# Causal attention with an int8 feed-forward on eight cores: scores and outputs issued in groups of two tiles, and VectorE's long work taken from a list

## The chip, the cores and the metric

One Trainium2 chip. The program runs on all 8 cores, each on one sequence of the batch, and no core waits for another. The time of a run is that of the slowest core, in device microseconds (us); a kernel's time is the median of its runs.

## What is computed

Per core, x is 2048 tokens by 1024 features. The reference, cut to one layer:

```
q = (x @ Wq.T) * 64 ** -0.5 ; k = x @ Wk.T ; v = x @ Wv.T      # 16 heads of 64
s = q @ k.T
attn = where(causal, 1 + s + 0.5 * s * s, 0)                   # no exponential
o = (attn @ v) / (attn.sum(-1) + 1e-6)
x = layernorm(x + o @ Wo.T)
x_scale = max(abs(x), -1) / 127 ; x_q = round(x / x_scale)
x = layernorm(x + (x_q @ weight_q.T) * x_scale * weight_scale + bias)
```

The kernel writes 1 + s + s²/2 as (s/√2 + 1/√2)² + 1/2: ScalarE squares the scores on their way out of PSUM, and the 1/2 comes in as a product of block sums of v with a step matrix.

## The kernel before

One Python program writes a queue of instructions for each engine; the engines run their queues in order and meet by semaphores. What stands earlier in an engine's queue is done earlier, so the order in which the program calls its functions is the schedule.

Attention runs in five stages, `GROUPS`: queries 0 to 511, 512 to 1023 and 1024 to 1535 (stages 0, 1, 2, width 512), then 1536 to 1791 and 1792 to 2047 (stages 3a and 3b, width 256). In each, 8 pairs of heads follow one another, and a pair has 3, 7, 11, 7 or 8 tiles of keys. A tile has two halves of TensorE work:

- `scores` (L458): two matmuls of 64 rows and up to 512 columns, one for each head of the pair, placed in the upper and the lower half of the array (`tile_position`), into one of two PSUM tiles `ps`. ScalarE's square (L470) empties it into `u`, one of 4 buffers. Tiles on the diagonal, up to three for a pair, get a causal mask from VectorE (L477), called 1.0 us of planned time later.
- `outputs` (L514): two matmuls of 128 rows onto `oab`, preceded on a pair's first tile by the constant's (L497). After a pair's last tile `finish` copies `oab` out (L572, L573, L576), sends the row sums through SP's DMAs for a reciprocal and a broadcast (L578 to L593), and GpSimd multiplies (L597).

The outputs of tile j are issued behind the scores of tile j+3 (`LOOK`). Between them `drive` puts other TensorE work, the filling: the projections of the next stage (K, Q, V items), and for the stage before the output projection (`out_proj`, item a), the transposes of its integers (`turn`, t) and the feed-forward (`ffn`, f). All are groups of 8 matmuls of 512 columns (`mm8`, L288) into two PSUM banks `fb`, which VectorE empties: the eviction. An order written out by hand, `orders`, lists the items of each stage, and `drive` hands them out two matmuls ("slots") at a time, in proportion to the tiles done; after a pair's last outputs `END_FILL` lets 4 more through.

Work that must come some time later is entered in `later` by `at(delay, fn)` against a planned clock, which gains `STEP_US` for a tile and `SLOT_US` for a slot. `run_until` takes entries out early when something needs them. After `out_proj(t)` VectorE runs the largest and smallest of each row (L669, L670), then for a pair of tiles short statistics (`chain1`), a root on ScalarE, `scales`, and the integers of both tiles (L721, `quantize`); `turn` adds bias (L749), `ffn` empties its banks with two operations a half (L768, L772); `chain2`, a root and `final` (L805) end with the store. All of these enter VectorE's queue at the call.

After stage 3b the last two tiles, 14 and 15, go through the same steps in a tail that is written out by hand.

Of the kernel before, what the change touches and what calls it, by code (L numbers as in the profile page):

```python
# [39 lines left out]
LOOK = 3  # L40
END_FILL = 4
NB = 6
STEP_US = 0.86
SLOT_US = 0.215
QRING = 8
NX1 = 4
# [70 lines left out]
def build_nc():  # L117
# [185 lines left out]
    def proj_qk(c, p, which):  # L303
# [25 lines left out]
        bank["free"][bi] = tok  # L329

    def proj_v(c, tt, half):
# [17 lines left out]
        bank["free"][bi] = tok  # L349

# [35 lines left out]
    clock = {"now": 0.0, "n": 0}  # L386
# [7 lines left out]
    def run_later():  # L394
        while later and later[0][0] <= clock["now"]:
            later.pop(0)[2]()

    def run_until(there):
        while not there():
            clock["now"] = max(clock["now"], later[0][0])  # L400
            later.pop(0)[2]()

# [30 lines left out]
    def attention(grp):  # L433
# [171 lines left out]

        for j in range(len(seq) + LOOK):
            if j < len(seq):
                scores(*seq[j])
            if j >= LOOK:
                outputs(*seq[j - LOOK])  # L610

            yield END_FILL if width == 512 and j >= LOOK and seq[j - LOOK][1] == seq[j - LOOK][2] - 1 else 0
# [25 lines left out]
    def load_tile(t):  # L638
        buf, b = home(t)
        if t < NT - 4:  # L640
            run_until(lambda: t >= NX1 or t + 2 in t_norm)
            waits = [t_out.get(t - NX1), t_norm[t + 2] if t < NX1 else None]
        else:
            waits = [t_vdone[0]]
# [10 lines left out]
    def out_proj(t):  # L655
# [3 lines left out]
        for half in range(2):  # L659
# [9 lines left out]
        P.op("vector", lambda e: e.reduce_max(MX(t, t + 1), buf[:, :], AX.X), [tok], inc=False)  # L669
        t_chain[t] = P.op("vector", lambda e: e.tensor_reduce(  # L670
            MN(t, t + 1), buf[:, :], AX.X, ALU.min))

        def square():
# [3 lines left out]
            if t % 2:  # L677
                at(3.5, lambda: chain1(t - 1, 2))
# [3 lines left out]
    def chain1(t0, n):  # L682
# [12 lines left out]
        def root():  # L695
            ts = P.op("scalar", lambda e: e.activation(
                V1(a, b), V1(a, b), AF.Sqrt, bias=c_eps), [tv])
            at(1.8, lambda: scales(ts, t))
# [16 lines left out]
    def quantize():  # L715

        while quant[0] in t_mm2 and (quant[0] < 2 or quant[0] - 2 in t_tr):
            k = quant[0]
            quant[0] += 1
            buf, _ = home(k)  # L720
            t_xq[k] = P.op("vector", lambda e, k=k, buf=buf: e.tensor_scalar(  # L721
                xq[k % 2][:, :], buf[:, :], S2(k, k + 1), MM2(k, k + 1), ALU.mult, ALU.add),
                [t_mm2[k], t_tr.get(k - 2)])

    def turn(t):
# [16 lines left out]
        def back():  # L742
# [6 lines left out]
        t_xb[t] = P.op("vector", lambda e: e.scalar_tensor_tensor(  # L749
            buf[:, :], buf[:, :], V1(t, t + 1), biasb[:, :], ALU.mult, ALU.add),  # L750
            [t_xq[t], tok_c["biasb"]])

    def ffn(t):
# [3 lines left out]
        for half in range(2):  # L757
# [9 lines left out]
            xh = buf[:, half * 512:(half + 1) * 512]  # L767
            t1 = P.op("vector", lambda e, bk=bk, half=half: e.scalar_tensor_tensor(  # L768
# [5 lines left out]
            bank["free"][bi] = tok  # L774
        t_r2[t] = tok

        def square():
# [3 lines left out]
            if t % 2:  # L781
                at(2.5, lambda: chain2(t - 1, 2))
# [3 lines left out]
    def chain2(t0, n):  # L786
# [9 lines left out]
        def root():  # L796
            ts = P.op("scalar", lambda e: e.activation(
                D1(a, b), D1(a, b), AF.Sqrt, bias=c_eps), [tv])
            at(1.0, lambda: final(ts))

        def final(ts):
            t = V(lambda e: e.reciprocal(D1(a, b), D1(a, b)), [ts])
            for k in range(a, b):
                buf, bf = home(k)
                tf = P.op("vector", lambda e, k=k, buf=buf: e.tensor_scalar(  # L805
                    buf[:, :], buf[:, :], M1(k, k + 1), D1(k, k + 1), ALU.subtract, ALU.mult), [t])
                t_out[k] = P.dma("sync", lambda e, k=k, buf=buf: e.dma_start(
                    d_out[k * 128:(k + 1) * 128, :], buf[:, :]), sem_ou[bf], [tf])
# [47 lines left out]
    def drive(main, steps, fill, total):  # L856
# [3 lines left out]
        for i, more in enumerate(main):  # L860
            clock["now"] += STEP_US
            run_later()
            while live and given < total * (i + 1) / steps + more:
# [39 lines left out]
    for grp, (c, first, width) in enumerate(GROUPS):  # L903
# [3 lines left out]
        steps = NP * len(u_tiles(c, first, width)) + LOOK  # L907
# [8 lines left out]
    run_until(lambda: not later)  # L916
# [208 lines left out]
```

How the kernel before makes its waits and increments, by code:

```python
        def play(eng, todo):  # L101
            for waits, fn, sem, k in todo:
                for s, v in waits:
                    eng.wait_ge(s.h, v)
                inst = fn(eng)
                if sem is not None:
                    inst.then_inc(sem.h, k)
```

## Time and profile before

| | |
|---|---|
| median of 3 runs | 662.59 us (655.40 to 665.08) |
| profiled execution | 665.16 us |
| its span, slowest core (core 2) | 663.6 us |
| other cores | 642.6 to 656.3 us |
| TensorE matmul busy | 601.0 us (91%), 3335 matmuls |
| TensorE weight load | 246.0 us (37%) |
| ScalarE busy | 371.2 us (56%) |
| VectorE busy | 344.2 us (52%) |
| mean granted clock, core 2 | 0.929 |

The span runs from the first instruction of a core to its last; the profiled execution's own time has about 1.5 us around it. A matmul's end is modelled and reaches over the next one's start, so TensorE's real pace is read from one start to the next. Stage 0 begins at 72 us on core 2, stage 1 at 151, stage 2 at 302, 3a at 452, 3b at 531 and ends at about 623.

### The profile page before, as it was taken

The numbers are of one execution on the slowest core, as the hardware profiler recorded it, in microseconds if no ns is written. First come the engines' busy times: TensorE is split into PE (matmuls) and PEld (weight loads), VectorE is DVE, ScalarE is ACT, GpSimd is POOL, SyncE is SP. The second block draws the span as 40 slices with busy tenths as digits, with TensorE's granted clock in tenths as the row PEclk, the third lists the DMA queues.
The fourth block names the chain that finished last, engine by engine and source line by source line (L and its number), as shares of the span: only waits on it lengthen the run. The fifth ranks groups of instructions, "written<-read, shape, count | busy, mean of one in ns | idle before, by whom it ended". The sixth has DMA issues, their size and how long they took to land.

```text
span 663.6 us, 10428 instructions; the slowest of 8 cores (642.6 to 663.6 us)
## 1 busy us (share of the span) xinstructions
PE 601.0 (91%) x3335; PEld 246.0 (37%) x3335; DVE 344.2 (52%) x773; ACT 371.2 (56%) x419; POOL 101.5 (15%) x147
## 2 busy tenths in 40 slices
PE   2989999999689889999999989999999978989973
PEld 0333333343223324333333333334445434444531
DVE  0324344553146766642376756453467744564585
ACT  0000333324336557546677768767889778998533
POOL 9100111121411111123210100012000120000000
PEclk9988888888769889999999989999999979999998
DMA  8996297725751224457721002133100140002011
GB/s 108 162 153 103 34 131 102 129 62 136 157 122 57 65 48 110 104 112 126 196 43 40 16 25 89 39 90 120 52 20 25 49 178 13 19 22 81 21 64 64
DMA packets 34276, 54.53 MB, mean 82 GB/s; under 512 B 10736, under 2 KB 13616, under 8 KB 34224
## 3 DMA queue, kind: packets, MB, share of 16 engines
q0 software_dynamic: 14976, 31.46, 26.8%
q1 hardware_dynamic: 19248, 22.41, 11.5%
q8 instruction: 28, 0.46, 0.3%
q14 instruction: 24, 0.20, 0.1%
HBM read 61.00 MB, written 8.52 MB: 105 GB/s over the span
## 4 chain that ended last, share of the span: by engine, by line
PE 61%; DMA 13%; DVE 10%; issue 7%; ACT 4%; SPq 3%; POOL 2%; DVEq 0%; ACTq 0%; POOLq 0%
PE fb L288 30%; PE oab L514 16%; PE ps L458 11%; DMA wv_sb<-wv 4%; DMA zscr<-zg 4%; DMA zg<-x 2%; PE oab L497 2%; ACT u L470 2%; DMA rzb<-zscr 2%; DMA zg<-osb 1%; DVE fb L768 1%; DVE xq L721 1%; SPq L593 1%; DVE u L477 1%; POOL wk_sb L230 1%
## 5 line engine op out<-in xcount | busy, mean ns | idle before, releaser
L470 ACT ACTIVATE u<-ps,consts 128x1024 f16<-128x1024 f32 (+2 forms) x288 | 303.5, 1066 | 173.1 <-PE ps L458 170.5
L514 PE MATMUL oab<-u,vx 128*128 128x256 f16 (+3 forms) x864 | 175.7, 311 | 1.1 <-DVE u L477 1.1
L458 PE MATMUL ps<-qT,kT 64*128 64x256 f16 (+3 forms) x864 | 112.5, 312 | 1.0 <-ACT u L470 0.7
L477 DVE SCALAR_TENSOR_TENSOR u<-u,cst_sb 128x256 f16<-128x256 f16 (+1 forms) x88 | 51.9, 591 | 79.4 <-ACT u L470 79.1
L514 PEld LDWEIGHTS oab<-u,vx 128*128 128x128 f16 x864 | 63.4, 99 | 63.8 <-issue 53.5
L597 POOL TENSOR_TENSOR slot<-osb,rzb 128x512 f16<-128x512 f32 (+1 forms) x35 | 39.2, 1120 | 291.8 <-DMA rzb<-zscr 278.9
L288 PE MATMUL fb<-wv_sb,slot 128*128 128x512 f16 x256 | 70.6, 414 | 6.2 <-DMA wv_sb<-wv 4.1
L458 PEld LDWEIGHTS ps<-qT,kT 64*128 64x128 f16 x864 | 30.5, 94 | 123.2 <-issue 122.1
L288 PE MATMUL fb<-wo_sb,slot 128*128 128x512 f16 x224 | 64.7, 397 | 11.7 <-POOL slot L597 8.4
L288 PE MATMUL fb<-wf_sb,xqT 128*128 128x512 f16 x224 | 63.0, 388 | 9.3 <-DVE stat L792 3.6
L288 PE MATMUL fb<-slot,wr 128*128 128x512 f16 x256 | 69.9, 394 | 1.4 <-DVE qT L326 1.4
L288 PE MATMUL fb<-slot,wk_sb 128*128 128x512 f16 x128 | 35.6, 431 | 13.0 <-DMA slot<-xT 12.7
L321 DVE CAST kT<-fb 128x512 f16<-128x512 f32 x32 | 22.1, 689 | 44.8 <-PE fb L288 44.7
L470 ACT ACT_TABLE_LOAD x1 | 1.3, 1283 | 72.7 <-PE ps L458 72.7
L288 PEld LDWEIGHTS fb<-wv_sb,slot 128*128 128x128 f16 x256 | 26.3, 104 | 40.9 <-issue 26.6
L288 PE MATMUL fb<-slot,wq_sb 128*128 128x512 f16 x128 | 36.2, 436 | 0.7 <-DVE qT L326 0.6
L288 PEld LDWEIGHTS fb<-slot,wr 128*128 128x128 f16 x256 | 24.7, 100 | 29.5 <-issue 12.5
L288 PEld LDWEIGHTS fb<-wo_sb,slot 128*128 128x128 f16 x224 | 22.5, 101 | 30.8 <-issue 19.2
L326 DVE TENSOR_SCALAR qT<-fb 128x512 f16<-128x512 f32 x32 | 21.9, 684 | 18.9 <-PE fb L288 18.6
L288 PEld LDWEIGHTS fb<-wf_sb,xqT 128*128 128x128 f16 x224 | 21.5, 99 | 25.6 <-issue 11.9
L666 DVE SCALAR_TENSOR_TENSOR x<-fb,x 128x512 f32<-128x512 f32 x24 | 16.5, 688 | 26.9 <-PE fb L288 26.8
L573 DVE COPY osb<-oab 128x512 f32<-128x512 f32 x20 | 13.8, 691 | 24.3 <-PE oab L514 21.2
(146 smaller groups left out, 521.5 us busy)
## 6 DMA issues: line engine op xcount, KB each, us to landing
rzb<-zscr SPq DMA_DIRECT2D x48, 128.0 KB, 2.9
x<-x_tok POOLq DMA_DIRECT2D x12, 512.0 KB, 7.7
out<-x SPq DMA_DIRECT2D x12, 512.0 KB, 3.4
slot<-xT POOLq DMA_DIRECT2D x16, 256.0 KB, 7.9
wr<-wk POOLq DMA_DIRECT2D x16, 256.0 KB, 5.3
wr<-wq POOLq DMA_DIRECT2D x16, 256.0 KB, 6.4
osb<-osb SPq DMA_DIRECT2D x20, 128.0 KB, 2.3
wk_sb<-wk POOLq DMA_DIRECT2D x8, 256.0 KB, 14.8
```

The lines of the kernel that those rows point to most:

```text
L230: tok_w[(0, name, j)] = tok_w[(1, name, j)] = P.dma("gpsimd", lambda e: e.dma_start(dst[:, j * D:(j + 1) * D], src[j]), s)
L288: tok = P.op("tensor", lambda e, lhs=lhs, rhs=rhs, i=i: e.matmul(out, lhs, rhs, start=(i == 0), stop=(i == n - 1)), list(w) + (list(waits) ...
L321: tok = P.op("vector", lambda e: e.tensor_copy(dst, bk[:, :]), [box[0]])
L326: tok = P.op("vector", lambda e: e.tensor_scalar(dst, bk[:, :], QSCALE, None, ALU.mult), [box[0], t_slast.get(c * NP + p - QRING)])
L458: tok = P.op("tensor", lambda e, r=r, kt=kt, qo=qo, w=w, col=col, ab=ab: e.matmul(pt[:, ab * 512 + col: ab * 512 + col + w], kT[r:r + 64, ...
L470: tok = P.op("scalar", lambda e: e.activation(dst, src, AF.Square, bias=c_rs, scale=RSQRT2), [t_s[g], t_o.get(g - NU), t_const])
L477: t_u[g] = P.op("vector", lambda e: e.scalar_tensor_tensor(ud, ud, 0.5, tri2[:, None, 0:diag].broadcast_to([128, 2, diag]), ALU.add, ALU.m ...
L497: t_oconst[c] = P.op("tensor", lambda e, ab=ab, base=base: e.matmul(oab[:, at_ab[ab]: at_ab[ab] + width], bs[c % 2][:, base: base + 128], ...
L514: tok = P.op("tensor", lambda e, base=base, qo=qo, w=w, col=col, ab=ab, end=end: e.matmul(oab[:, at_ab[ab] + qo: at_ab[ab] + qo + w], vx[: ...
L573: tb = t_oev[1] = P.op("vector", lambda e: e.tensor_copy(osb[b][:, 512:1024], oab[:, 512:1024]), [tok, before])
L597: t_norm[k] = P.op("gpsimd", lambda e: e.tensor_tensor(slot[o_slot[c]][:, p * 512 + first: p * 512 + first + width], osb[b][:, 0:width], r ...
L666: tok = P.op("vector", lambda e, bk=bk, xh=xh, acc=acc: e.scalar_tensor_tensor(xh, bk, 1.0, xh, ALU.mult, ALU.add, accum_out=acc), [box[0] ...
```

## The change

Tiles of one pair of heads are taken in groups of two (the last is alone where their number is odd). A group's scores are issued together, then the filling for both, then the outputs of the group before. `LOOK` and `END_FILL` are gone. VectorE's long operations, and the short statistics at each end of ScalarE's root except `root` itself, go into a second list, `idle`, in order of a rank; each eviction of the filling takes one entry out behind it, and so does a planned 2.2 us in which none was taken. The store of each tile is now split from its neighbour's, `load_tile` waits in the program until the buffer's store has been issued, and a planned tile costs 0.76 us instead of 0.86.

```
 NU = 4
-LOOK = 3
-END_FILL = 4
 NB = 6
-STEP_US = 0.86
+STEP_US = 0.76
 SLOT_US = 0.215
+IDLE_US = 2.2
 QRING = 8
...
         bank["free"][bi] = tok
+        evicted()
...
         bank["free"][bi] = tok
+        evicted()
...
-    clock = {"now": 0.0, "n": 0}
+    clock = {"now": 0.0, "n": 0, "idle": 0.0}
     later = []
...
             later.pop(0)[2]()
+        if idle and clock["now"] - clock["idle"] >= IDLE_US:
+            run_idle()
...
         while not there():
+            if idle and (not later or later[0][0] > clock["now"]):
+                run_idle()
+                continue
             clock["now"] = max(clock["now"], later[0][0])
...
+    idle = []
+    def when_idle(rank, fn):
+        idle.append((rank, clock["n"], fn))
+        clock["n"] += 1
+        idle.sort(key=lambda x: x[:2])
+    def run_idle():
+        clock["idle"] = clock["now"]
+        idle.pop(0)[2]()
+    def evicted():
+        if idle:
+            run_idle()
...
-        for j in range(len(seq) + LOOK):
-            if j < len(seq):
-                scores(*seq[j])
-            if j >= LOOK:
-                outputs(*seq[j - LOOK])
-            yield END_FILL if width == 512 and j >= LOOK and seq[j - LOOK][1] == seq[j - LOOK][2] - 1 else 0
+        groups = []
+        for p in range(NP):
+            mine = [x for x in seq if x[0] == p]
+            groups += [mine[i:i + 2] for i in range(0, len(mine), 2)]
+        before = []
+        for group in groups:
+            for x in group:
+                scores(*x)
+            yield len(group)
+            for x in before:
+                outputs(*x)
+            before = group
+        for x in before:
+            outputs(*x)
...
         if t < NT - 4:
-            run_until(lambda: t >= NX1 or t + 2 in t_norm)
+            run_until(lambda: t - NX1 in t_out if t >= NX1 else t + 2 in t_norm)
             waits = [t_out.get(t - NX1), t_norm[t + 2] if t < NX1 else None]
...
             bank["free"][bi] = tok
-        P.op("vector", lambda e: e.reduce_max(MX(t, t + 1), buf[:, :], AX.X), [tok], inc=False)
-        t_chain[t] = P.op("vector", lambda e: e.tensor_reduce(
-            MN(t, t + 1), buf[:, :], AX.X, ALU.min))
+            if half == 0:
+                evicted()
+        def largest():
+            P.op("vector", lambda e: e.reduce_max(MX(t, t + 1), buf[:, :], AX.X), [tok], inc=False)
+        def smallest():
+            t_chain[t] = P.op("vector", lambda e: e.tensor_reduce(
+                MN(t, t + 1), buf[:, :], AX.X, ALU.min), [tok])
+            if t % 2:
+                if t in t_sq1:
+                    when_idle(0, lambda: chain1(t - 1, 2))
+        when_idle(0, largest)
+        when_idle(0, smallest)
+        evicted()
...
             t_junk[0] = t_sq1[t]
-            if t % 2:
-                at(3.5, lambda: chain1(t - 1, 2))
+            if t % 2 and t in t_chain:
+                at(1.2, lambda: when_idle(0, lambda: chain1(t - 1, 2)))
...
                 V1(a, b), V1(a, b), AF.Sqrt, bias=c_eps), [tv])
-            at(1.8, lambda: scales(ts, t))
+            at(1.8, lambda: when_idle(0, lambda: scales(ts, t)))
...
             quant[0] += 1
-            buf, _ = home(k)
-            t_xq[k] = P.op("vector", lambda e, k=k, buf=buf: e.tensor_scalar(
-                xq[k % 2][:, :], buf[:, :], S2(k, k + 1), MM2(k, k + 1), ALU.mult, ALU.add),
-                [t_mm2[k], t_tr.get(k - 2)])
+            def integers(k=k):
+                buf, _ = home(k)
+                t_xq[k] = P.op("vector", lambda e: e.tensor_scalar(
+                    xq[k % 2][:, :], buf[:, :], S2(k, k + 1), MM2(k, k + 1), ALU.mult, ALU.add),
+                    [t_mm2[k], t_tr.get(k - 2)])
+            when_idle(0, integers)
...
         at(0.5, back)
-        t_xb[t] = P.op("vector", lambda e: e.scalar_tensor_tensor(
-            buf[:, :], buf[:, :], V1(t, t + 1), biasb[:, :], ALU.mult, ALU.add),
-            [t_xq[t], tok_c["biasb"]])
+        def bias():
+            t_xb[t] = P.op("vector", lambda e: e.scalar_tensor_tensor(
+                buf[:, :], buf[:, :], V1(t, t + 1), biasb[:, :], ALU.mult, ALU.add),
+                [t_xq[t], tok_c["biasb"]])
+        when_idle(1, bias)
...
             xh = buf[:, half * 512:(half + 1) * 512]
+            run_until(lambda: t in t_xb)
             t1 = P.op("vector", lambda e, bk=bk, half=half: e.scalar_tensor_tensor(
...
             bank["free"][bi] = tok
+            evicted()
         t_r2[t] = tok
...
             if t % 2:
-                at(2.5, lambda: chain2(t - 1, 2))
+                at(1.2, lambda: when_idle(2, lambda: chain2(t - 1, 2)))
...
                 D1(a, b), D1(a, b), AF.Sqrt, bias=c_eps), [tv])
-            at(1.0, lambda: final(ts))
-        def final(ts):
-            t = V(lambda e: e.reciprocal(D1(a, b), D1(a, b)), [ts])
             for k in range(a, b):
-                buf, bf = home(k)
-                tf = P.op("vector", lambda e, k=k, buf=buf: e.tensor_scalar(
-                    buf[:, :], buf[:, :], M1(k, k + 1), D1(k, k + 1), ALU.subtract, ALU.mult), [t])
-                t_out[k] = P.dma("sync", lambda e, k=k, buf=buf: e.dma_start(
-                    d_out[k * 128:(k + 1) * 128, :], buf[:, :]), sem_ou[bf], [tf])
+                at(1.0, lambda k=k: when_idle(2, lambda: final(k, ts)))
+        def final(k, ts):
+            t = V(lambda e: e.reciprocal(D1(k, k + 1), D1(k, k + 1)), [ts])
+            buf, bf = home(k)
+            tf = P.op("vector", lambda e: e.tensor_scalar(
+                buf[:, :], buf[:, :], M1(k, k + 1), D1(k, k + 1), ALU.subtract, ALU.mult), [t])
+            t_out[k] = P.dma("sync", lambda e: e.dma_start(
+                d_out[k * 128:(k + 1) * 128, :], buf[:, :]), sem_ou[bf], [tf])
...
         live = True
-        for i, more in enumerate(main):
-            clock["now"] += STEP_US
+        made = 0
+        for n in main:
+            made += n
+            clock["now"] += STEP_US * n
             run_later()
-            while live and given < total * (i + 1) / steps + more:
+            while live and given < total * made / steps:
                 w = next(fill, None)
...
         total = sum(cost.get(it[0], 0) for it in orders[grp].split())
-        steps = NP * len(u_tiles(c, first, width)) + LOOK
+        steps = NP * len(u_tiles(c, first, width))
         drive(attention(grp), steps if grp < len(GROUPS) - 1 else steps - 8, phase(c, orders[grp]), total)
...
     bank["n"] = 0
-    run_until(lambda: not later)
+    run_until(lambda: not later and not idle)
     V = lambda fn, w=(): P.op("vector", fn, w)
```

## Rows read from the trace of the kernel before

**Rows 1.** Spans and mean granted clock, three of the eight cores.
```profile
core 2: 663.6 us, clock 0.929
core 3: 656.3 us, clock 0.934
core 4: 642.6 us, clock 0.968
```

**Rows 2.** Core 2 by stage: stretch, length, busy us of each engine.
```profile
72.00:151.00 79.00, 78.97 (x355) 30.63 (x355) 40.32 (x83) 28.52 (x33) 15.17 (x23) 0.81 0.61 96
190.00:302.00 112.00, 104.98 (x522) 40.32 (x521) 71.53 (x168) 62.08 (x75) 19.06 (x25) 0.94 0.37 84
302.00:452.00 150.00, 145.16 (x738) 52.65 (x738) 82.94 (x180) 109.75 (x120) 20.27 (x23) 0.99 0.29 71
452.00:531.00 79.00, 78.27 (x617) 38.57 (x616) 45.67 (x106) 66.10 (x72) 9.48 (x12) 1.00 0.18 56
531.00:614.00 83.00, 74.46 (x586) 35.74 (x584) 43.35 (x97) 70.90 (x77) 7.02 (x10) 0.96 0.18 62
```

**Rows 3.** Timeline of TensorE: start, us, line, shapes, count.
```profile
306.65 0.59 PE L288 MATMUL fb<-slot,wr 128*128 128x512 f16 x2
307.18 0.39 PE L458 MATMUL ps<-qT,kT 64*128 64x512 f16 x2
307.50 0.60 PE L514 MATMUL oab<-u,vx 128*128 128x512 f16 x2
...
307.95 1.03 PE L288 MATMUL fb<-slot,wr 128*128 128x512 f16 x4
308.91 0.39 PE L458 MATMUL ps<-qT,kT 64*128 64x512 f16 x2
...
316.56 0.39 PE L458 MATMUL ps<-qT,kT 64*128 64x128 f16 x4
316.88 0.39 PE L514 MATMUL oab<-u,vx 128*128 128x512 f16 x1
```

**Rows 4.** What TensorE waited for: us in total, times, longest.
```profile
PE fb L288 <- POOL slot L597: 8.4, 2, 8.1
PE fb L288 <- DVE vx L347: 4.8, 4, 2.4
PE fb L288 <- DVE stat L792: 3.6, 1, 3.6
PE fb L288 <- ACT xqT L743: 3.0, 2, 1.6
PE fb L288 <- DVE x L772: 2.9, 2, 1.9
```

**Rows 5.** Timeline: VectorE's integers, an eviction behind them, TensorE's wait.
```profile
216.96 1.53 DVE L721 TENSOR_SCALAR xq<-x,stat 128x1024 f16<-128x1024 f32 x2
...
218.42 0.42 DVE L346 CAST vx<-fb 128x256 f16<-128x256 f32 x1
...
219.31 2.10 PE L288 MATMUL fb<-wo_sb,slot 128*128 128x512 f16 x7 [2.36 <-DVE vx L347]
```

**Rows 6.** The stretch after that wait, granted clock behind POOL's column.
```profile
220.40:223.80 3.40, 3.40 (x10) 0.94 (x9) 1.76 (x3) 1.11 (x1) 1.26 (x1) 0.50 0.22 54
```

**Rows 7.** Core 4: the last norm of group 0 and TensorE (timeline).
```profile
167.96 1.26 POOL L597 TENSOR_TENSOR slot<-osb,rzb 128x512 f16<-128x512 f32 x1 [5.59 <-DMA rzb<-zscr]
...
169.36 0.58 PE L288 MATMUL fb<-wo_sb,slot 128*128 128x512 f16 x1 [6.55 <-POOL slot L597]
```

**Rows 8.** ScalarE's squares, grouped by form: busy, mean ns, idle before.
```profile
L470 ACT ACTIVATE u<-ps,consts 128x1024 f16<-128x1024 f32 x248 | 273.9, 1114 | 150.8 <-PE ps L458 148.8 <-PE oab L514 0.6
```

**Rows 9.** VectorE's masks, grouped by form.
```profile
L477 DVE SCALAR_TENSOR_TENSOR u<-u,cst_sb 128x256 f16<-128x256 f16 x48 | 23.2, 483 | 48.6 <-ACT u L470 48.3
```

**Rows 10.** Timeline: integers of tiles 12 and 13, first transposes.
```profile
585.60 1.54 DVE L721 TENSOR_SCALAR xq<-x1l,stat 128x1024 f16<-128x1024 f32 x2
...
586.56 0.38 PE L732 MATMUL fb<-cst_sb,xq 128*128 128x128 f16 x4 [0.27 <-DVE xq L721]
```

## Prediction, made before the changed kernel ran

> **What bounds the kernel now.** I read the spans first: core 2 ends last at 663.6 us with a mean granted clock of 0.929, core 4 needs 642.6 at 0.968 [rows 1]. The difference arises early. Core 2 is granted 0.81 from 72 to 151 us [rows 2], and the cores come together again at a wait that no TensorE work shortens: the output projection of stage 0 needs the norm of the last pair of heads, whose DMAs land late. On core 4 GpSimd waits 5.59 us for them and TensorE 6.55 us in the last of its waits there, and it goes on at 169.4 us [rows 7]; core 2, which comes later, still waits 8.1 us [rows 4]. So TensorE time saved ahead of that point (185 us on core 2) is given back.
>
> Behind it, by the table of stages, TensorE is busy 105 of 112, 145 of 150, 78 of 79 and 74 of 83 us [rows 2]. ScalarE is next: 110 of 150 us in stage 2, 66 of 79 in 3a and 71 of 83 in 3b. VectorE never passes 72 of 112. TensorE bounds the kernel from 185 to about 614 us, and ScalarE is near enough in stage 3 to limit what TensorE can gain.
>
> What TensorE spends is in the timeline [rows 3]. Two filling matmuls take 306.65 to 307.18, 0.53 us; four take 307.95 to 308.91, 0.96 us. So one takes 0.215 us, and each run of them that ends in scores 0.10 us on top. The scores take 0.32 us (307.18 to 307.50, 308.91 to 309.23). Their two matmuls lie in different halves of the array and overlap, so the pass itself is one matmul long, 0.215, and 0.105 is on top again. The four score matmuls from 316.56, 512 columns in each half, also take 0.32: within scores nothing is paid for the next matmul. The pattern is a toll of about 0.105 us at each change between half-array and whole-array matmuls, in both directions; the table of instructions shows none of it as idle.
>
> The Trainium skill, page TensorEngine Tiling (Array Packing), section Key Properties, says that changing the tiling mode, not just the tile, drains TensorE. The trace agrees, with 0.10 and 0.11 us; without that rule the same rows could be a cost of each score tile, and grouping would save nothing (a rival, below).
>
> **Part 1, groups of two.** A pair has 3, 7, 11, 7, 8 tiles and gets 2, 4, 6, 4, 4 groups. Changes of mode before: 2 x 8 x 36 = 576. After: 2 x 8 x 20 = 320. Removed by stage: 16, 48, 80, 48, 64. At 0.105 us: 1.7, 5.0, 8.4, 5.0, 6.7, in sum 26.9 us. What of it counts:
> - stage 0 and the first 10 or so of stage 1's 56 tiles lie ahead of the wait for the norm: 0. Rest of stage 1: 46/56 x 5.0 = 4.1.
> - stage 2: 8.4. ScalarE stays at 110 of some 140 us.
> - stage 3a: ScalarE's 66 us fit in 79 - 5 = 74, but at 89% a queue of two squares will sometimes be late: 4.5.
> - stage 3b: the last pair has no filling; there a tile is 0.32 + 0.10 + 0.43 = 0.85 us of TensorE against 1.11 us of a square [rows 8], so its 8 changes are worth nothing. Of the other 56 x 0.105 = 5.9 I take 5.0.
> That makes 22.0, between 12.5 (stage 3 wholly at ScalarE's pace) and 24.3.
>
> Does the new order wait for squares? A group's second scores need the square of the preceding group's second tile. From those scores' end to that need TensorE has the filling, two outputs and one score tile: 1.3 us plus the filling. ScalarE needs both squares, 2.2 us, less the 0.2 by which it began earlier, plus some 0.2 of hand-over: 2.2. So the filling must last 0.9 us for a group. Stage 1 has 340 slots for 56 tiles, 2.6 us a group; stage 2 308 for 88, 1.5; 3a 132 for 56, 1.0; 3b 104 for 56, 0.8. No wait in 1 and 2, about none in 3a, a short one in 3b, which I count in the 5.0.
>
> **Part 2, masks.** For widths of 512 the last three tiles of a pair are masked, and two of them now share a group. Both masks enter VectorE's queue ahead of the group's filling, and the second waits for the second square. Behind it wait that filling's evictions, and behind those TensorE, once it needs the bank again, 8 slots later. Before, VectorE stood for one square less. That is up to 1.11 us [rows 8] for each of the 16 pairs of stages 1 and 2 (the 8 of stage 0 are ahead of the wait): 0 to 18 us, and no gain is possible, as no mask comes earlier. Masks already wait 48.6 us for ScalarE in 48 cases [rows 9] and TensorE's waits on evictions lie elsewhere, so the banks mostly cover one square: I take 0.2 us each, 3 us. Outputs of the group follow both fillings and four tiles' matmuls, over 3 us later, and need nothing new. Without `END_FILL` the copy of `oab` is covered by the next pair's two scores and their filling, over 1.4 us in stages 1 and 2, against 0.7 of a copy; in stage 3 the pairs alternate banks. Cost 0.
>
> **Part 3, the list.** TensorE waits 4.8 us for L347 and 2.9 for L772 [rows 4]; the transposes' wait for L772, a smaller row of that view, brings 2.1. One is shown: the integers of two tiles hold VectorE from 216.96 for 1.53 us, the eviction starts at 218.42, and TensorE had stood 2.36 us at 219.31 [rows 5]. A list with one entry behind each eviction splits such rows of work: of 9.8 us I take 6, with 0 and 9.8 as ends. The 3.6 and 3.0 us [rows 4] end with the copy of the transposes, which stands on ScalarE behind squares: not touched. Behind the gap of rows 5 the granted clock is 0.50 for 3.4 us [rows 6], which costs 1.7; with those at 240.9 and 384.3 us three such stretches follow VectorE's gaps, 5.1 us, of which I take half, 2.6. Added are 7 reciprocals of some 0.15 us on VectorE, beside other work. The loads of tiles 4 to 11 on GpSimd's queue (and the ring's loads behind them) now wait in the program for the store; it has been issued long before in all of them, so 0. SP gets the same stores, one by one. The tail is the same code; up to two `final` fall ahead of it, beside TensorE's projection: 0, at most 1.6 us.
>
> **Sum.** 22.0 - 3 + 6 + 2.6 = 27.6 us off the profiled 665.2: 637.6. The profiled execution lies 2.6 us above the median of the runs shown, so a median might be 635; I say 637.
>
> **Rivals.**
> - The list is late. Each entry costs up to 2.2 us of planned delay. Between a pair's last eviction in `out_proj` and its integers stand four of them, 8.8 us. For tiles 12 and 13 there is no slack now: the first transposes wait 0.27 us for the integers [rows 10]. 8.8 there and half as much at two or three more pairs is some 20 us. For it: the rows. Against it: `run_until` takes the entries out when `turn` needs them, so only real work remains late. Time 637 + 20 = 657, no change by measurement.
> - Masks at their full price, 15 us more, or stage 3 wholly at ScalarE's pace, 9.5 us more: 647 to 652.
> - The toll belongs to each score tile and not to the change of mode. Against it: the four matmuls at 316.56. Then 22.0 falls away: 659.
> - Slower: the clock. Core 2 shows 0.81 from 72 to 151 us, where TensorE's matmuls follow one another without gaps [rows 2], and pays little for it, since the wait for the norm swallows it. The change makes stages 1 and 2 denser. If the same grant held through both, 262 us of which I put 210 down to matmul passes (the 250 busy, less tolls and waits within), each longer by 23%, it would cost 48 us: 685. It decides from 13 + 27.6 = 41 us of cost, that is from about 175 us of such passes. Against it: core 2 was granted 0.99 through stage 2 with TensorE busy 145 of 150 us. The Trainium skill, page TensorE: Matmul & The Clock Gate, section Part 1: The HAM clock gate, says that three cores of a die in dense matmuls take the whole die to 13/16. This trace does not agree: of all cores only 2 and 3, of one die, fall to 0.93 on the mean [rows 1]. By that rule alone the middle stages would already run at 0.81 and the change would leave the clock alone.
>
> **How the numbers follow.** Chances: forecast 0.63 (624 to 648), late list 0.12, masks or ScalarE 0.10, toll not saved 0.04, clock 0.06, and 0.05 for something better than counted, down to 616. A measurement of this kernel tells changes from about 2% on, 649 and 676 us. Faster by more: 0.63 + 0.05 + part of the masks = 0.72; within 2%: 0.19; slower: 0.09. The lower end takes all tolls, all waits and all clock (24.3 + 9.8 + 5.1 = 39) from the median: 623. The upper end reaches into the late list: 660.
>
> **What would show it.** Score matmuls in runs of two tiles, 0.53 us together, with 0.10 before; stage 2 near 141 us; 3a near 74; no matmul waiting over 1 us on L347 or L772; the wait for the norm longer by 1 to 3 us. Wrong if integers come after TensorE is ready for them, if VectorE stands on masks with two full banks, or if any core of the second half of the span shows 0.81.

## The result, and the profile after

The changed kernel is slower: 682.97 us median of 4 runs (670.94 to 693.44) against 663.84 (655.40 to 666.04) for the kernel before. The forecast was 637.

In most runs of either kernel the cores of one pair or one die were granted less clock than the rest and ended last; the ratio of the runs least touched by this is 1.023 (95% interval 1.014 to 1.032), and experiments are compared by "full-grant spans", the median span over all cores, of all runs of a kernel, whose mean granted clock was 0.945 or more. By that measure the kernel before takes 648.1 us (154 cores of the 27 runs made beside the experiments) and the changed one 666.3 us (23 cores of 4 runs): +18 us, near the 19 us by which the medians differ. The traces below are of core 6, which was not held back in either profile. Its spans, before and then after:

```profile
core 6: 649.7 us, clock 0.968
```

```profile
core 6: 661.1 us, clock 0.956
```

The stages of core 6 before, from behind the wait for the last norm of stage 0 (stretch, length, busy time of TensorE, its weight load, VectorE, ScalarE, GpSimd, then the granted clock, the DMA share and GB/s; the same columns as [rows 2]):

```profile
175.00:292.00 117.00, 104.82 (x534) 41.04 (x535) 73.70 (x171) 63.23 (x77) 19.85 (x26) 0.96 0.43 91
292.00:441.00 149.00, 143.16 (x737) 52.35 (x735) 81.82 (x180) 109.35 (x120) 19.86 (x23) 1.00 0.30 72
441.00:519.00 78.00, 77.77 (x612) 38.25 (x608) 45.00 (x105) 65.93 (x71) 8.42 (x12) 1.00 0.18 57
519.00:610.00 91.00, 81.79 (x667) 40.70 (x664) 46.33 (x105) 78.18 (x85) 7.80 (x11) 0.98 0.18 59
```

and after:

```profile
172.00:289.00 117.00, 101.26 (x539) 40.95 (x540) 72.86 (x172) 61.47 (x76) 19.72 (x27) 0.98 0.36 83
289.00:440.00 151.00, 139.35 (x741) 53.95 (x742) 82.97 (x184) 106.60 (x122) 19.16 (x22) 0.98 0.29 70
440.00:520.00 80.00, 76.19 (x614) 41.52 (x613) 44.63 (x103) 64.82 (x71) 9.45 (x13) 0.98 0.18 55
520.00:622.00 102.00, 83.51 (x665) 47.07 (x662) 45.84 (x108) 75.89 (x85) 7.72 (x11) 0.90 0.16 53
```

TensorE's busy time falls in stages 1, 2 and 3a, as it should, and the stages get no shorter: idle time has taken its place. Stage 3b is 11 us longer, at a granted clock of 0.90. Its 11 us can be added up from the profile, as medians over the cores without 0.81: TensorE's waits (gaps over 0.15 us) grow from 9.2 to 18.6 us, the time at a granted clock of 0.50 grows from 3.4 to 20.5 us, and half of that growth, 8.5 us, is lost, as matmuls take twice as long there; the tolls give 6.7 back.

The tolls themselves are gone, as the timeline of the changed kernel shows (the answer to [rows 3]):

```profile
314.48 1.03 PE L537 MATMUL oab<-u,vx 128*128 128x512 f16 x4
315.44 0.61 PE L481 MATMUL ps<-qT,kT 64*128 64x512 f16 x4
315.98 0.82 PE L287 MATMUL fb<-wo_sb,slot 128*128 128x512 f16 x3
```

Two score tiles take 0.54 us (315.44 to 315.98) where they took 0.32 each, and the toll of 0.1 us in front of them (four outputs, 0.96 us) is paid once.

What has grown stands in the waits of VectorE. Before:

```profile
DVE u L477 <- ACT u L470: 71.8, 54, 4.6
```

After:

```profile
DVE u L500 <- ACT u L493: 126.1, 70, 5.2
```

That is the mask line: VectorE stands 54 us longer in front of masks whose squares aren't done. What this does to TensorE can be seen in a piece of the changed kernel's timeline, in stage 0, where the list is still empty:

```profile
118.26 0.50 PE L481 MATMUL ps<-qT,kT 64*128 64x512 f16 x4
...
118.76 1.69 ACT L493 ACTIVATE u<-ps,consts 128x1024 f16<-128x1024 f32 x2 [3.64 <-PE ps L481]
...
119.97 1.65 DVE L500 SCALAR_TENSOR_TENSOR u<-u,cst_sb 128x256 f16<-128x256 f16 x2 [2.31 <-ACT u L493]
...
121.66 0.69 DVE L325 TENSOR_SCALAR qT<-fb 128x512 f16<-128x512 f32 x1
...
122.50 0.81 PE L287 MATMUL fb<-slot,wq_sb 128*128 128x512 f16 x3 [1.78 <-DVE qT L325]
```

Both masks of the group stand ahead of the eviction at L325; VectorE waits 2.31 us for the first square, and TensorE, out of banks, 1.78 us for the eviction. With two squares ahead of everything on ScalarE and a list entry in front of an eviction, such a wait grows. In stage 2:

```profile
354.17 1.70 ACT L493 ACTIVATE u<-ps,consts 128x1024 f16<-128x1024 f32 x2
...
355.40 0.43 DVE L500 SCALAR_TENSOR_TENSOR u<-u,cst_sb 128x256 f16<-128x256 f16 x1 [3.06 <-ACT u L493]
...
358.72 0.43 DVE L346 CAST vx<-fb 128x256 f16<-128x256 f32 x1
...
359.62 1.86 PE L287 MATMUL fb<-wf_sb,xqT 128*128 128x512 f16 x4 [4.58 <-DVE vx L347]
```

VectorE stood 3.06 us for a square, then ran both masks and, from 356.32 to 358.78, a row of short statistics, and the eviction came at 358.72. So of TensorE's 4.58 us some 2.4 are the statistics, an entry of the list. Its next four matmuls take 1.86 us instead of 0.96: after the gap the granted clock is 0.50.

### The profile page after: what moved, and what is told of

Read it like the earlier page. It is cut to its first block, busy times and chain, and to the rows that moved or that the text cites. A ratio compares the mean times of both kernels' runs of the same rounds, so it can differ in the third digit from the quotient of the medians.

```text
span 688.3 us, 10452 instructions; the slowest of 8 cores (661.1 to 688.3 us)
## 1 busy us (share of the span) xinstructions
PE 586.4 (85%) x3335; PEld 255.7 (37%) x3335; DVE 343.9 (50%) x780; ACT 361.0 (52%) x419; POOL 98.4 (14%) x147
## 4 chain that ended last, share of the span: by engine, by line
PE 56%; DMA 12%; DVE 12%; issue 9%; ACT 8%; POOL 2%; SPq 1%; DVEq 0%; ACTq 0%; POOLq 0%
PE fb L287 30%; PE oab L537 14%; PE ps L481 9%; ACT u L493 6%; DMA zscr<-zg 5%; DMA wv_sb<-wv 4%; DMA rzb<-zscr 2%; PE oab L520 2%; DMA zg<-osb 2%; DVE fb L822 1%; DVE u L500 1%; DVE qT L325 1%; PE fb L781 1%; DVE xq L768 1%; ACT xqT L792 1%
## 5 line engine op out<-in xcount | busy, mean ns | idle before, releaser
L493 ACT ACTIVATE u<-ps,consts 128x1024 f16<-128x1024 f32 (+2 forms) x288 | 292.5, 1065 | 160.1 <-PE ps L481 159.3
L537 PE MATMUL oab<-u,vx 128*128 128x256 f16 (+3 forms) x864 | 154.7, 311 | 2.9 <-DVE u L500 2.4
L537 PEld LDWEIGHTS oab<-u,vx 128*128 128x128 f16 x864 | 83.4, 101 | 62.2 <-issue 20.9
L481 PE MATMUL ps<-qT,kT 64*128 64x256 f16 (+3 forms) x864 | 95.5, 311 | 5.5 <-ACT u L493 5.0
L287 PE MATMUL fb<-wv_sb,slot 128*128 128x512 f16 x256 | 67.7, 408 | 10.3 <-DMA wv_sb<-wv 4.5
L287 PE MATMUL fb<-wo_sb,slot 128*128 128x512 f16 x224 | 59.9, 395 | 18.5 <-POOL slot L620 17.3
L287 PE MATMUL fb<-slot,wr 128*128 128x512 f16 x256 | 67.2, 400 | 2.0 <-DVE qT L325 1.8
L287 PEld LDWEIGHTS fb<-wf_sb,xqT 128*128 128x128 f16 x224 | 18.7, 101 | 51.9 <-issue 39.3
L287 PEld LDWEIGHTS fb<-wo_sb,slot 128*128 128x128 f16 x224 | 19.1, 100 | 49.0 <-issue 35.4
L287 PEld LDWEIGHTS fb<-slot,wr 128*128 128x128 f16 x256 | 22.8, 101 | 38.0 <-issue 24.2
L595 ACT COPY osb<-oab 128x512 f32<-128x512 f32 x20 | 11.7, 585 | 40.0 <-PE oab L537 28.7
L325 DVE TENSOR_SCALAR qT<-fb 128x512 f16<-128x512 f32 x32 | 21.8, 686 | 21.7 <-PE fb L287 21.6
```

Of the source, the lines that this page charges most:

```text
L287: tok = P.op("tensor", lambda e, lhs=lhs, rhs=rhs, i=i: e.matmul(out, lhs, rhs, start=(i == 0), stop=(i == n - 1)), list(w) + (list(waits) ...
L325: tok = P.op("vector", lambda e: e.tensor_scalar(dst, bk[:, :], QSCALE, None, ALU.mult), [box[0], t_slast.get(c * NP + p - QRING)])
L481: tok = P.op("tensor", lambda e, r=r, kt=kt, qo=qo, w=w, col=col, ab=ab: e.matmul(pt[:, ab * 512 + col: ab * 512 + col + w], kT[r:r + 64, ...
L493: tok = P.op("scalar", lambda e: e.activation(dst, src, AF.Square, bias=c_rs, scale=RSQRT2), [t_s[g], t_o.get(g - NU), t_const])
L537: tok = P.op("tensor", lambda e, base=base, qo=qo, w=w, col=col, ab=ab, end=end: e.matmul(oab[:, at_ab[ab] + qo: at_ab[ab] + qo + w], vx[: ...
L595: ta = t_oev[0] = P.op("scalar", lambda e: e.copy(osb[b][:, 0:512], oab[:, 0:512]), [tok, before])
```

## The experiments

All stage lengths below run from the first square of a stage to the first of the next, median over the cores of the profiled run that were never granted 0.81; 3b runs to its last square. Stage 1 is counted from the end of the last norm of stage 0 ("1, behind"). Full-grant spans are as above. How far they can be trusted: the kernel before, made anew on the three chips that the experiments ran on, takes 647.1, 648.5 and 648.0 us, and if the runs of a kernel are drawn anew from those that it has, its median mostly moves within 1 to 5 us (e2 from 645 to 652, e8 from 637 to 641.5, e12 from 637.6 to 639.8). The threshold of 0.945 also counts in favour of kernels with long gaps, as gaps lower the mean clock: e6 has only 13 cores above it. Steps of 1 or 2 us are therefore read from the stages and not from the spans, and the stages are those of one execution.

```
                      full-grant   stage 0   1, behind  stage 2   3a     3b
before                648.1        64.5      114.9      149.6     78.1   90.7
changed kernel        666.3        72.4      117.9      151.1     79.2   102.1
e1 groups only        672.3        71.8      118.2      153.9     81.8   100.1
e2 list only          646.6        64.5      112.7      146.2     78.0   93.9
e3 late masks         642.2        64.3      108.9      141.5     78.6   96.3
e4 no masks           637.8        63.8      107.0      142.0     77.9   96.6
e5 before, no masks   641.3        64.3      112.1      146.8     78.0   90.5
e6 groups, late masks 660.2        64.4      112.8      152.1     81.8   97.5
e7 second mask late   663.1        67.4      114.3      156.3     79.0   96.6
e8 hybrid             640.5        64.3      108.9      141.1     78.6   94.3
e9 half squares       630.5        64.3      108.8      141.8     73.7   87.9
e10 split groups      654.2        65.5      111.0      150.0     80.6   95.8
e11 list, late masks  645.3        64.3      113.1      146.6     78.2   94.5
e12 best              638.5        64.4      108.8      141.4     79.1   90.8
```

Three theories stood at the start. M: the masks of a group, issued ahead of its filling's evictions, hold VectorE, and TensorE runs out of banks. L: the list delays VectorE's chains by more than the groups win. F: the filling of a group, twice as long, outruns its two banks wherever it stands. The times expected for e1 to e4 are meant beside 663 us for the kernel before; beside its full-grant 648 only the differences can be compared.

### The two halves alone

Groups only: the loop over groups, `drive` and `STEP_US` of the changed kernel in the kernel before.

```diff
-        for j in range(len(seq) + LOOK):
...
+        for group in groups:
+            for x in group:
+                scores(*x)
+            yield len(group)
+            for x in before:
+                outputs(*x)
```

> Groups of two as in the changed kernel, with its planned tile of 0.76 us, but VectorE's long work enters its queue at the call, as before; no list. Theory M (masks): both masks of a group stand ahead of the filling's evictions, so VectorE's wait for squares at the mask line grows from 72 us to some 125 us as in the changed kernel, and the time is 670 to 680 us, close to the changed kernel. Theory L (the list loses what the groups win): groups alone save their tolls, 640 us. Theory F (a filling of double length outruns its two banks): like M in time, but with TensorE's waits on evictions in stages where no mask is near.

List only: the changed kernel with the old loop, `LOOK = 3`, `END_FILL = 4` and `STEP_US = 0.86`.

> The list of VectorE's long work as in the changed kernel, but tiles interleaved one by one as before (outputs three tiles behind their scores, 4 extra slots after a pair, planned tile 0.86 us). Theory M: the list is harmless or gains up to 6 us: 655 to 663 us, VectorE's wait for squares at the mask line near 72 us. Theory L: the list itself costs: 670 to 680 us, with waits of 4 to 5 us on transposes and evictions in stages 2 and 3b.

Groups alone cost 24 us (648.1 to 672.3), and the list alone changes nothing that the spans can tell (646.6). VectorE's wait at the mask line is 115.0 us in groups only (core 6). That speaks against L: the list is not what makes the kernel slow; it even takes 6 us off the groups. M and F are still even. Within list-only, stage 1 gains 2.2 us, stage 2 gains 3.4 and 3b loses 3.2. The groups come with three smaller edits that no run takes apart from them: a planned tile of 0.76 us instead of 0.86, and no `LOOK` and `END_FILL`.

### Masks later, and masks left out

```diff
-                at(1.0, mask)
+                at(2.6 + 1.1 * seat[0], mask)      # seat: 0 or 1, place in the group
```

> The changed kernel with one edit: the masks of a group are called 2.6 us and 3.7 us of planned time after the scores instead of 1.0, so that evictions due before the squares stand ahead of them in VectorE's queue. Theory M: VectorE's wait for squares at the mask line falls by some 40 us or more, TensorE's waits on evictions with it, and the time falls to 645 to 655 us. Theory L or F: within 5 us of the changed kernel, 670 or more.

> The changed kernel without the masks of diagonal tiles (the causal mask inside them is left out, so attention there is not the reference's). It takes VectorE's 88 masks of 0.6 us, 52 us of VectorE's busy time, and all its waits for squares away. Theory M: below the kernel before, 640 us or less. Theory L or F: some 5 to 8 us below the changed kernel, 665 us or more, as VectorE is idle half the time anyway.

Moving the masks by 1.6 and 2.7 us of planned time, and nothing else, brings the changed kernel from 666.3 to 642.2 us, 6 us below the kernel before (8 to 18 were expected). The filling is as long as it was, so theory F falls too. VectorE's wait at the mask line, core 6 of the kernel with late masks:

```profile
DVE u L501 <- ACT u L494: 38.9, 24, 5.1
```

126.1 us have become 38.9. What TensorE no longer waits for in stage 2 is the eviction, core 6 of the changed kernel:

```profile
PE fb L287 <- DVE vx L347: 4.6, 1, 4.6
PE oab L537 <- DVE u L500: 1.8, 1, 1.8
```

and of the kernel with late masks, where its longest wait of the stage is

```profile
PE oab L538 <- DVE u L501: 1.0, 1, 1.0
```

All its waits of the stage sum to 12.6 us in the changed kernel and 4.8 with late masks, and 6.8 us at a granted clock of 0.50 are gone. By stages the move gives 9.0 us in stage 1, 9.6 in stage 2, 0.6 in 3a and 5.8 in 3b, 25 in sum; the 8 us of stage 0 vanish too, but lie ahead of the norm, which ends at 177.4 us in the changed kernel and 174.3 with late masks (169 to 181 by core in the profiles, so those 3 us say little). Leaving the masks out altogether takes off only 4.5 us more. The size that I expected for that run was too large (22 us or more below the kernel before, 10.3 found), but the verdict is M's. In the kernel before, the same edit:

```diff
-            if diag:
+            if False:
```

> The kernel before without its diagonal masks (left out of the computation, so attention inside diagonal tiles is not the reference's). Theory M (the second mask of a group, standing ahead of evictions, is what the new order pays for): one tile at a time the banks cover the mask's wait, so this is at most 3 us below the kernel before, and the 28 us that separate the changed kernel with and without masks belong to the groups. Rival N (masks on VectorE cost as much in any order): 15 to 25 us below the kernel before.

In the kernel before the masks cost 7 us (648.1 to 641.3), more than the 3 I gave to M and far less than the 28.5 of the changed kernel. The difference, some 21 us, belongs to their place in the new order. This run also says what the whole change is worth when masks can't matter: 641.3 to 637.8, 3.5 us. So masks are not all of it; of 27 us of tolls most is lost elsewhere.

### Which mask

```diff
-                at(1.0, mask)
+                at(1.0 + 2.7 * seat[0], mask)
```

> The changed kernel with one edit: the first mask of a group at 1.0 us as it is, only the second at 3.7 us of planned time. Theory M in its narrow form, that only the second mask stands too early: the same as with both late, 642 us on cores at full grant, within 3 us. Rival: both stand too early, since the filling now begins right behind the scores: half way, 650 to 656 us.

The narrow form of M falls, and the rival's 650 to 656 us are not met either: 663.1 us, and VectorE's wait is still

```profile
DVE u L501 <- ACT u L494: 97.5, 48, 5.5
```

The first mask stands too early as well. In the old order outputs and filling were shared out around each tile and its mask entered the queue two matmuls into the filling; now the planned clock gains 1.52 us for both tiles before any filling is handed out, so that an entry at 1.0 us is due at once, and the filling begins right behind the scores, with the group's outputs after it. Only 3b agrees with the narrow form (102.1 to 96.6): there a pair has 8 tiles, and the one masked tile is always the second of its group. Stage 2 is even longer than in the changed kernel, by 5.2 us. The longest wait for an eviction is still there (core 7):

```profile
PE fb L287 <- DVE vx L347: 4.0, 1, 4.0
PE fb L287 <- POOL slot L621: 4.0, 1, 4.0
```

The second row is a norm. As means over the cores without 0.81, the norms cost TensorE 2.5 us in that stage against 1.5 in the changed kernel, the masks themselves 3.7 against 1.7, and the time at 0.50 is 11.9 against 6.8 us (medians), some 2.5 us of stream. These account for most of the 5 us; why they fall so is open.

### Groups with late masks, without the list

> Groups of two with late masks (2.6 and 3.7 us of planned time), and no list: VectorE's long work enters its queue at the call. With the list and the same late masks, cores at full grant took 642 us. Theory A (list and groups add up): the list is worth 1 to 6 us here too, so 643 to 648 us on such cores. Theory B (groups only work with the list, since a filling in one piece needs its evictions sooner): 655 us or more.

660.2 us, against 642.2 with the list: theory B. With late masks the list is worth 18 us to groups, and 2.8 us to single tiles (e11 against the kernel before). Stage 2 shows most of it (152.1 against 141.5). The reason given in theory B is not what the trace shows, though. In stage 2 the evictions cost TensorE 0.6 us; it waits for the masks, 9.0 us in four waits on core 6. The longest of them:

```profile
335.04 1.53 DVE L730 TENSOR_SCALAR xq<-x,stat 128x1024 f16<-128x1024 f32 x2
...
337.28 1.22 DVE L678 TENSOR_REDUCE stat<-x 128x1 f32<-128x1024 f32 x1
338.42 1.21 DVE L679 TENSOR_REDUCE stat<-x 128x1 f32<-128x1024 f32 x1
339.55 1.02 DVE L478 SCALAR_TENSOR_TENSOR u<-u,cst_sb 128x256 f16<-128x256 f16 x2
340.11 0.59 PE L515 MATMUL oab<-u,vx 128*128 128x256 f16 x2 [5.89 <-DVE u L478]
```

A late mask enters VectorE's queue behind whatever was called at once before it, here integers and two reductions, and the group's outputs stand for it. The list, which lets one such piece in at a time, is what makes late masks affordable. With it the same stage has 1.0 us of waits for masks.

### The toll

```diff
             for k, x in enumerate(group):
                 seat[0] = k
                 scores(*x)
-            yield len(group)
+                yield 1
```

with both masks at 2.2 us.

> The same kernel with late masks and list, but the filling of a group is divided: one half between its two score tiles, one half behind. Outputs stay in groups. It puts two changes between half-array and whole-array matmuls back for each group of two, 128 in 160 groups, so 256 changes, as before. Toll theory: the scores of a group no longer run on, 0.1 us at each change; stage 2 becomes 8.4 us longer, 141 to 149 or 150 us, stage 1 behind the wait by 4. Rival: the toll is not what groups gain, and stage 2 stays within 3 us of 141.

Stage 2 grows from 141.5 to 150.0 us, 8.5 us for the 80 changes of mode that it puts back, 0.106 us each at most: the masks moved as well, TensorE's waits grew from 4.8 to 5.6 us and 1.7 us fell to a granted clock of 0.50, so some 7 us, 0.09 each, are left for the toll. The cleaner price is the timeline's. TensorE's timeline of this kernel, core 7, shows the toll back around each score tile:

```profile
332.09 0.39 PE L482 MATMUL ps<-qT,kT 64*128 64x512 f16 x2
332.42 1.04 PE L287 MATMUL fb<-wo_sb,slot 128*128 128x512 f16 x4
333.38 0.28 PE L482 MATMUL ps<-qT,kT 64*128 64x256 f16 x2
```

0.33 us for a full score tile (332.09 to 332.42) and 0.96 for four filling matmuls (332.42 to 333.38). Stage 1 grows by 2.1 of the 4 expected. By the Trainium skill's TensorEngine Tiling (Array Packing), Key Properties, a change of mode drains the array and a change of tile doesn't; this run and the row of 0.54 us for two tiles agree.

### Stage 3

```diff
+            sq = cols if width == 512 else cols // 2
-            src = pt[:, :].rearrange("p (a w) -> p a w", a=2)[:, :, 0:cols]
+            src = pt[:, :].rearrange("p (a w) -> p a w", a=2)[:, :, 0:sq]
...
```

> The list, groups of two and late masks, with ScalarE's squares of stages 3a and 3b cut to half their columns (the other half of each tile of u keeps old contents, so attention there is not the reference's). ScalarE's square falls from 1.11 to some 0.65 us there; TensorE's work is unchanged. Theory S (ScalarE's pace of 1.1 us a square and its queue ate the tolls in stage 3): 3a falls from 78.6 to 73 or 74 us, 3b from 96.3 to below 90. Rival R (the latency of VectorE's chain and of the norms sets stage 3): 3a stays within 2 us of 78, 3b within 3 us of 96.

With squares of half the columns 3a falls from 78.6 to 73.7 us, the 5 us that the tolls amount to there, and 3b from 96.3 to 87.9. So in 3a ScalarE took what TensorE saved. In 3b 8.4 us are more than its tolls (6.7 us); how much of the gain is the tolls is not shown, as the kernel before was not run with half squares. The hybrid goes back to single tiles there:

```diff
+        if width == 256:
+            for j in range(len(seq) + 3):
+                seat[0] = -1                    # mask at 1.0 us, as before
+                if j < len(seq):
+                    scores(*seq[j])
+                if j >= 3:
+                    outputs(*seq[j - 3])
+                yield 1
+            return
```

> List and late masks with groups of two in stages 0 to 2, and one tile at a time in stages 3a and 3b, as before (masks there at 1.0 us, planned tile 0.86 us). Theory S (in stage 3 ScalarE sets the pace, and two squares ahead of each copy of the transposes cost more than the tolls give): 3a stays at 78 us, 3b falls from 96 to 91 to 94 us; 637 to 640 us on cores at full grant, the fastest so far. Rival (tolls count in stage 3 too): 3a and 3b no shorter than with groups, 642 us or more.

3a is the same either way, 3b falls by 2.0 us, and the span of 640.5 lies at the edge of what was expected. One row of waits shows what groups cost in 3b. Kernel with late masks, core 1:

```profile
570.10 1.91 ACT L494 ACTIVATE u<-ps,consts 128x1024 f16<-128x1024 f32 x2 [0.27 <-PE ps L482]
570.25 0.62 PE L783 MATMUL fb<-cst_sb,xq 128*128 128x128 f16 x8
...
571.89 1.02 ACT L794 ACTIVATE xqT<-fb 128x1024 f16<-128x1024 f16 x1
...
573.17 0.71 PE L287 MATMUL fb<-wf_sb,xqT 128*128 128x512 f16 x2 [2.31 <-ACT xqT L794]
```

The transposes end at about 570.9; their copy stands behind two squares instead of one, and the feed-forward, next in TensorE's queue, waits 2.31 us.

### What single tiles gain from late masks, and the best version

> The list with tiles one at a time, as in the list-only run, and masks called 1.9 us of planned time after the scores instead of 1.0. The kernel before without masks was 7 us faster than with them at full grant. If a mask called behind its square costs next to nothing, this is 641 us on cores at full grant, as good as groups of two with late masks (642), with stage 2 at 143 to 146 and stage 3b at 92 to 94; groups are then worth only stage 2's tolls. If masks cost their busy time whatever their place, 645 to 647.

645.3 us against 646.6, and stage 2 146.6 against 146.2: nothing that can be told. With single tiles a mask's place, 1.0 or 1.9 us, doesn't matter. Beside the hybrid this run also says what groups are worth in stages 1 and 2 once the masks stand well: 4.2 and 5.5 us by stages (113.1 to 108.9 and 146.6 to 141.1), 4.8 us by the spans.

The best version is the hybrid with stage 3's masks at 1.9 us and, in 3b, no list:

```diff
+        if grp == 4:
+            while idle:
+                run_idle()
+            at_once[0] = True                   # when_idle calls at once from here on
```

> A version meant to beat both: list, groups of two and late masks in stages 0 to 2; one tile at a time in 3a and 3b with masks at 1.9 us of planned time; and no list in 3b, where VectorE's long work enters its queue at the call. 3b should fall from 94 to 90 or 91 us, since the list-only run had 94 there against 91 before: 637 us on cores at full grant, against 640.5 with the list in 3b. If the list did not cause those 3 us, it stays at 640.

3b falls from 94.3 to 90.8 us, the length of the kernel before, so the list was what cost 3b those 3.5 us (the masks moved too, which in 3b alone gave nothing: 93.9 and 94.5 us in e2 and e11). Its profiled run, all cores at full grant, took 643.42 us with spans of 635.1 to 641.9; the full-grant span is 638.5 us, against 648.1 before and 666.3 for the changed kernel, a gain of 1.5%. The plain medians are 658.16 us (5 runs) and 663.20 us for the kernel before beside it (7 runs), 0.8% apart, with no interval.

## Why the prediction was wrong

- **The step that failed is part 2, the masks.** It had the mechanism, and mis-sized the term. I took 0.2 us for each of 16 pairs, 3 us, with 18 as the upper end, since "TensorE's waits on evictions lie elsewhere, so the banks mostly cover one square". The move of the masks measured 9.0 and 9.6 us in stages 1 and 2: 18.6, the upper end itself. Before, the banks covered the wait because the filling was spread over tiles; in one piece it is not covered, as stage 0 shows with an empty list. And I missed 3b: 8 tiles make the one masked tile the second of its group, 5.8 us. In sum 25 us for 3. The row that reassured me, [rows 9], was also misread: its 48 counts masks of one shape and not waits, and with the other shape VectorE's idle time ahead of masks was 79 us and not 48.6.
- **The masks are about half of the miss.** By full-grant spans the change was to take 27.6 us off and added 18.2, 46 us apart. The masks are 22 of it. The rest is missing with late masks too: stage 3 was to become 9.5 us shorter and became longer, by 0.5 us in 3a and 5.6 in 3b, some 16 us apart, and the list and its clock gave little of their 8.6.
- **The toll's price was right, its worth was not.** The score pair takes 0.54 us where I gave 0.53, and putting the tolls of stage 2 back costs 8.5 us (some 7 without the longer waits) where I had 8.4. But grouping gains 4.2 and 5.5 us in stages 1 and 2 against single tiles with the list, where I had 4.1 and 8.4: in the larger stage a third of it is missing, 1.3 us of that to longer waits (4.5 against 3.2 us, e8 and e11). The upper end of 24.3 us in part 1 doesn't add up either: 4.1 + 8.4 + 5.0 + 5.9 is 23.4, and 24.2 with the last pair that I had ruled out.
- **Stage 3 was over-sized.** 4.5 and 5.0 us forecast; with late masks groups gained nothing in 3a and cost 2 us in 3b against single tiles (e8). My own lower end (ScalarE's pace, nothing left) was the case, and half squares give 73.7 us where I had forecast 74. The estimate (a group's filling must last 0.9 us, and it lasts 1.0 us in 3a and 0.8 in 3b) left no room for the copies of transposes and the other squares on ScalarE.
- **The list.** 6 us and 2.6 us of clock forecast. Alone it gains 2.2 and 3.4 us in stages 1 and 2 and loses 3.2 in 3b, 1.5 by the span. The rival of the late list is real in 3b (e12 gives 3.5 us back), not the 20 us priced. Its sign came: in 3b of the changed kernel TensorE waits 4.1 us for integers (core 6). But that wait is 5.1 us in groups without the list and 1.7 in the list without groups, so the groups brought most of it. What I didn't see is that late masks in groups need the list (18 us).
- **"Not touched" was wrong for the copy of the transposes:** two squares now stand ahead of it, one more than before.
- **The wait for the norm** took stage 0's loss as it would have taken a gain: stage 0 takes 72.4 us instead of 64.5, and the last norm ends at 177.4 against 177.6.
- **The clock rival** did not decide: the full-grant cores carry the loss, though in the profiled runs four cores were granted 0.81 for 135 us after the change and two before. But gaps cost twice. Stretches at a granted clock of 0.50 sum to 63 us on a core of the changed kernel against 50 before (median of the cores as in the table, whole span), some 6.6 us of stream.

The sum for the changed kernel, against the kernel before and behind the norm: stage 1 +3.0, stage 2 +1.5, 3a +1.1, 3b +11.4, 17 us of the 18.

## What to carry to other kernels

Before reordering one engine's queue, list what waits in the other queues by program order, and place each such instruction behind the event it needs: in the same order of tiles the same masks cost 28 us or 4 us by where they were called. But a late call is only safe if nothing long can slip in ahead of it. In this kernel half-array and whole-array matmuls side by side pay about 0.1 us at each change, which no busy or idle column shows; grouping paid in the stages where ScalarE, which empties PSUM, had room, and not in 3a and 3b, where it was at 85% before. A wait priced with bounds 0 to 18 should be taken near the lower one only if a row shows its cover in the new order, not in the old.

## What the runs showed of the hardware

After the gap of 4.58 us in the timeline above the granted clock is 0.50, and four matmuls take 1.86 us instead of 0.96. In the profiled run of the changed kernel cores 2 to 5 had means of 0.913 to 0.923 and the other four 0.944 or more. The Trainium skill, TensorE: Matmul & The Clock Gate, Part 1: The HAM clock gate, has a whole die held together; here, in this run as in the kernel before [rows 1], it was two cores of a die and not four: 2 and 3 before, those and 4 and 5 after. Other runs do show a whole die at a low grant: in the list-only run of 722.33 us cores 4 to 7 had means of 0.804 to 0.818 and the other four 0.929 or more.
